# A gated recurrence of 256 steps on one core: a loop of 64 turns of 4 steps in place of 32 turns of 8

## What is computed

```python
h = silu(cond @ W1.T + b1)
gate = sigmoid(h @ W2.T + b2)[:, None, :]
# Haar levels up and down, every coefficient times gate: gives gate * x
x = x + (x + gate * x)
def step(prev_h, xw):
    next_h = tanh(prev_h @ Wh + xw)
    return next_h, next_h
xW = einsum('ntd,dh->nth', x, Wx) + b        # x: the scaled x of above
h_t = scan(step, h0=cond, xs=xW)             # 256 steps, one after the other
out = x + h_t
```

## Time and profile before

| | us |
|---|---|
| median of 3 runs (lowest, highest) | 200.63 (199.9, 201.95) |
| the profiled execution, its own time | 200.03 |
| its span, first to last instruction | 198.2 |
| TensorE matmul busy | 183.2 |
| ScalarE busy | 77.2 |
| VectorE busy | 83.0 |

### The profile page before, as it was taken

The page is one execution under the profiler, slowest core; times in us unless marked ns, Lnnn a source line. Parts: engine busy times, 40 slices in busy tenths (PEclk is TensorE's granted clock), DMA queues, the critical chain, the costliest instruction groups (busy, mean ns, idle before and its releaser), DMA issues.

```text
span 198.2 us, 25465 instructions
## 1 busy us (share of the span) xinstructions
PE 183.2 (92%) x12218; PEld 151.3 (76%) x12218; DVE 83.0 (42%) x267; ACT 77.2 (39%) x520; POOL 0.5 (0%) x5
## 2 busy tenths in 40 slices
PE   7776999999999999999999999999999999999996
PEld 4665888777778877777887777788777778887775
DVE  1632444444435344444434343444434343444441
ACT  4222333444444333444444433344444433334442
POOL 1000000000000000000000000000000000000000
DMA  5403999942002020201102020110202010020212
GB/s 161 168 7 88 318 408 416 379 197 106 0 26 80 0 107 0 106 0 45 61 0 106 2 107 0 61 45 0 106 0 106 0 77 31 0 106 0 107 53 53
DMA packets 6961, 17.99 MB, mean 91 GB/s; under 512 B 1443, under 2 KB 2726, under 8 KB 6950
## 3 DMA queue, kind: packets, MB, share of 16 engines
q1 hardware_dynamic: 6800, 17.71, 24.0%
q10 hardware_dynamic: 150, 0.15, 0.2%
HBM read 9.48 MB, written 8.39 MB: 90 GB/s over the span
## 4 chain that ended last, share of the span: by engine, by line
PE 90%; ACT 3%; issue 2%; DMA 2%; SPq 1%
PE bank_e L185 54%; PE bank_l L185 36%; ACT h_ring L172 3%; DMA wh_sb<-in_wh 2%; SPq L125 0%; SPq L124 0%; SPq L123 0%; SPq L122 0%
## 5 line engine op out<-in xcount | busy, mean ns | idle before, releaser
L185 PE MATMUL bank_e<-h_ring,wh_sb 128*32 128x32 f32 x4096 | 101.5, 201 | 8.1 <-ACT h_ring L172 8.1
L185 PEld LDWEIGHTS bank_e<-h_ring,wh_sb 128*32 128x32 f32 x4096 | 72.9, 110 | 37.6 <-ACT h_ring L172 24.4
L185 PE MATMUL bank_l<-h_ring,wh_sb 128*32 128x32 f32 x4096 | 96.2, 196 | 1.8 <-issue 1.8
L172 ACT ACTIVATE h_ring<-bank_e 128x32 f32<-128x32 f32 x256 | 50.6, 198 | 115.0 <-PE bank_e L185 115.0
L315 DVE TENSOR_TENSOR x<-x,h_ring 128x128 f32<-128x128 f32 x129 | 37.6, 291 | 106.0 <-ACT h_ring L172 106.0
L185 PEld LDWEIGHTS bank_l<-h_ring,wh_sb 128*32 128x32 f32 x4096 | 74.6, 113 | 1.9 <-issue 1.9
L185 PE MATMUL bank_l<-x_ring,wx_sb 128*32 128x64 f32 x2080 | 66.3, 224 | 0.7 <-issue 0.7
L185 PE MATMUL bank_e<-x_ring,wx_sb 128*32 128x128 f32 x1040 | 57.4, 282 | 0.0
L172 ACT ACTIVATE h_ring<-bank_l 128x32 f32<-128x32 f32 x256 | 50.2, 196 | 0.2 <-PE bank_l L185 0.2
L185 PEld LDWEIGHTS bank_l<-x_ring,wx_sb 128*32 128x32 f32 x2080 | 46.4, 111 | 0.9 <-issue 0.8
L185 PE MATMUL bank_l<-ones,b_parts 128*32 128x64 bf16 x520 | 31.6, 194 | 0.0
(11 more groups left out here) (25 smaller groups left out, 9.7 us busy)
## 6 DMA issues: line engine op xcount, KB each, us to landing
x<-in_x SPq DMA_DIRECT2D x15, 512.0 KB, 9.7
out_dram<-x SPq DMA_DIRECT2D x15, 512.0 KB, 3.0
x<-in_x SPq DMA_DIRECT2D x1, 384.0 KB, 5.0
w_t<-in_w SPq DMA_DIRECT2D x1, 256.0 KB, 3.2
wx_sb<-in_wx SPq DMA_DIRECT2D x1, 256.0 KB, 4.5
wh_sb<-in_wh SPq DMA_DIRECT2D x1, 256.0 KB, 4.5
out_dram<-x SPq DMA_DIRECT2D x1, 256.0 KB, 2.1
w_t<-in_w_cond SPq DMA_DIRECT2D x1, 145.0 KB, 2.8
```

Source lines behind the costliest of these rows:

```text
L172: nc.scalar.activation(h_ring[:, m, s * B:(s + 1) * B], z_of(s, m), ACT.Tanh)\
L185: done = nc.tensor.matmul(out[q:q + 32], weights[:, q:q + 32], moving, start=start, stop=stop, skip_group_check=True)
```

## The change

TURN is 4 and PART is 2: the loop has 64 turns of 4 steps, `x_ring` and `h_ring` hold 4 steps, and a part is 2 steps. `bank_l` has one bank for each of the 4 steps in place of two steps to a bank, so that second halves are laid one step (32 columns) at a time, and first halves 2 steps (64 columns) at a time. The pairs of fill in steps 0 to 3 are 0, 40, 32, 48. ScalarE waits, before every even step from step 4 on, until VectorE has added the h that it will overwrite. SyncE waits once, for h of step 4, and then issues chunks 1 to 15. VectorE's order within a turn is new. The first part of x that SyncE loads (`FIRST`) is 64 columns in place of 128.

```diff
-    TURN, PART = 8, 4
+    TURN, PART = 4, 2
...
             part, of = divmod(s, PART)
-            return bank_l[part][of % 2][:, of // 2 * B:(of // 2 + steps) * B] if m else \
-                bank_e[part][:, of * B:(of + steps) * B]
+            return bank_l[part][of][:, 0:B] if m else bank_e[part][:, of * B:(of + steps) * B]
...
+            sp.wait_ge(h_ready[0][1], 2)
             for c in range(1, CHUNKS):
-                if c == 1:
-                    sp.wait_ge(h_ready[6][1], 1)
-                if c == 2:
-                    sp.wait_ge(h_ready[0][1], 2)
                 sp.dma_start(x1[:, c, :, :], x[:, c, :, :]).then_inc(x_loaded[c], DMA)
...
             for t in range(T):
                 s = t % TURN
+
+                if t >= TURN and t % 2 == 0:
+                    act.wait_ge(out_ready, t // 2 - 1)
                 for m in range(HALVES):
                     act.wait_ge(z_whole[m], t + 1)
...
-            lay_bias(0, 4, 0, opens=False)
-            lay_bias(0, 2, 1, opens=False)
-            lay_bias(1, 2, 1)
+            lay_bias(0, 2, 0, opens=False)
+            lay_bias(0, 1, 1, opens=False)
+            lay_bias(1, 1, 1)
...
-                    done = lay_input(0, 2 if m else 4, k, m)
+                    done = lay_input(0, 1 if m else 2, k, m)
...
             def fill(s, turn):
                 if s == 1:
                     pe.wait_ge(input_ready[1], turn)
-                    lay_bias(4, 4, 0)
-                    lay_input(4, 4, 0, 0)
+                    for m in range(HALVES):
+                        lay_bias(2, 2 - m, m)
+                        lay_input(2, 2 - m, 0, m)
+                        lay_input(2, 2 - m, 1, m)
                 if s == 2:
-                    lay_input(4, 4, 1, 0)
-                    lay_bias(4, 2, 1)
+                    lay_bias(3, 1, 1)
+                    lay_input(3, 1, 0, 1)
+                    lay_input(3, 1, 1, 1)
+                    lay_bias(0, 2, 0)
+                    pe.wait_ge(input_ready[0], turn)
+                    lay_input(0, 2, 0, 0)
                 if s == 3:
-                    lay_input(4, 2, 0, 1)
-                    lay_input(4, 2, 1, 1)
-                    lay_bias(5, 2, 1)
...
+                    lay_input(0, 2, 1, 0)
+                    for at in range(PART):
+                        lay_bias(at, 1, 1)
+                        lay_input(at, 1, 0, 1)
+                        lay_input(at, 1, 1, 1)
...
             for turn in range(TURNS):
...
+                t = turn * TURN
+                more = turn + 1 < TURNS
+                dve.wait_ge(h_ready[0 if turn else 1][1], turn + 1)
+                if more:
+                    if (t + TURN) % CS == 0:
+                        dve.wait_ge(x_loaded[(t + TURN) // CS], DMA)
+                    scale(turn + 1, 0, in_place=False).then_inc(input_ready[0], 1)
+                else:
+                    nc.vector.memset(x_ring[:, :, 0:PART * B], 0.0).then_inc(input_ready[0], 1)
+                dve.wait_ge(x1_ready, 2 * turn + 1)
+                dve.wait_ge(h_ready[1][1], turn + 1)
+                add_out(t)
+                if more:
+                    dve.wait_ge(input_ready[0], turn + 1)
+                    scale(turn + 1, 0, in_place=True).then_inc(x1_ready, 1)
+                dve.wait_ge(x1_ready, 2 * turn + 2)
+                if more:
+                    dve.wait_ge(h_ready[3][1], turn + 1)
+                    add_out(t + 2)
+                    scale(turn + 1, 1, in_place=False).then_inc(input_ready[1], 1)
+                    dve.wait_ge(input_ready[1], turn + 2)
+                    scale(turn + 1, 1, in_place=True).then_inc(x1_ready, 1)
```

More of the change, by code:

```diff
@@ L204, in lay_input @@
             def lay_input(s, steps, k, m):
[L205 to L208, removed]
+                return by_columns(z_of(s, m, steps), wx_sb[:, k, m * P:(m + 1) * P],
+                                  x_ring[:, k, s * B:(s + steps) * B])
             def recur(s, k, m, h, start=False):
@@ L244, in _ @@
                         pe.wait_ge(first_input_ready, k + 1)
-                    done = lay_input(0, 2 if m else 4, k, m)
+                    done = lay_input(0, 1 if m else 2, k, m)
                 done.then_inc(z_whole[m], 1)
             for k in range(HALVES):
-                lay_input(1, 2, k, 1)
+                lay_input(1, 1, k, 1)
             def fill(s, turn):
@@ L254, in fill @@
                     pe.wait_ge(input_ready[1], turn)
-                    lay_bias(4, 4, 0)
-                    lay_input(4, 4, 0, 0)
+                    for m in range(HALVES):
+                        lay_bias(2, 2 - m, m)
+                        lay_input(2, 2 - m, 0, m)
+                        lay_input(2, 2 - m, 1, m)
                 if s == 2:
-                    lay_input(4, 4, 1, 0)
-                    lay_bias(4, 2, 1)
-                if s == 3:
-                    lay_input(4, 2, 0, 1)
-                    lay_input(4, 2, 1, 1)
-                    lay_bias(5, 2, 1)
[L264 to L279, removed]
+                    lay_bias(3, 1, 1)
[4 more added lines that the diff above has]
+                    lay_input(0, 2, 0, 0)
+                if s == 3:
+                    lay_input(0, 2, 1, 0)
[3 more added lines that the diff above has]
+                        lay_input(at, 1, 1, 1)
             with nc.Fori(1, TURNS + 1, engines=bass.OrderedEngineSet([pe.engine]), head_slot={pe.engine: 0}) as turn:
@@ L349, in _ @@
             for turn in range(TURNS):
[L350 to L374, removed]
@@ new lines, in _ @@
+                dve.wait_ge(h_ready[1][1], turn + 1)
[10 more added lines that the diff above has]
+                    scale(turn + 1, 1, in_place=True).then_inc(x1_ready, 1)
+                else:
+                    dve.wait_ge(h_ready[2][1], TURNS)
+                    add_out(t + 2, steps=1)
+                    dve.wait_ge(h_ready[3][0], TURNS)
+                    dve.wait_ge(h_ready[3][1], TURNS)
+                    add_out(t + 3, steps=1)
```

## The result

The changed kernel takes 208.63 us (median of 6 runs, 206.96 to 209.54), the kernel before, run beside it, 200.25 (199.9 to 201.95). The ratio is 1.039, with an interval of 1.035 to 1.043. The forecast was 200.5, up to 204.2. The profiled execution took 206.96 us, the shortest of the six, with a span of 205.1; what follows explains the 6.9 us by which this span exceeds the 198.2 of before. What made the other five up to 2.5 us longer has no trace.

What follows compares the result with a forecast made beforehand. It took the chain from first-half tanh through the recurrence, 0.718 us per step, as the bound. 200.03 - 1.35 (start) + 1.3 (fills) gave 200.0 us, stated as 200.5 for the median; range 198.6 to 204.2.

Steps and rivals of the forecast that it cites:

- The step that failed: ScalarE before even steps: the added wait on out_ready is met early and falls into 0.43 us of idling; cost nothing.
- its signs of being wrong: Listed signs against the forecast: four equal periods at 0.718, a step over 0.76, ScalarE waiting for VectorE, a loop-edge gap.
- The fills: TensorE's input and bias pairs between recurrences: two of every four steps tight, 0.01 us each, +1.3 us in all.
- the fills just fit: Rival, TensorE between recurrences: narrow bias costs half, only the start counts, 199.3 us; chance 0.22.
- The trailing group: TensorE's fourth column group in wide fills: trails by 0.07 us, so the next recurrence's last group is about 0.02 late.
- recurrence unqueued: Rival, recurrence behind fill(1) and fill(3): its loads no longer wait ready, 0.035 us per tight step, 203.7 us; chance 0.21.
- The start: The loop's first turn: one instruction-fetch gap of some 1.4 us in place of two, step 6 1.35 us earlier.
- The edges: Turn ends of the loop: 32 more of them, covered, cost nothing; without cover up to 0.3 us each.
- the cover: Time to spare at a turn's end between TensorE's compare and move and the next recurrence: 0.15 us, unchanged.
- VectorE's waits and chunk 1: VectorE's scales and adds ready in time, cover 0.35 us at the tightest; chunk 1 there near 18, wanted near 19.9.
- The added pairs: TensorE's fills: 120 pairs per 4 steps in place of 120 per 8, priced only through the fills' length.
- The 8 narrow pairs: TensorE's fills: 8 pairs with 32 f32 columns take 0.063 us.

Runs made afterwards that it cites:

- kernel 1: The changed kernel with ScalarE's two waits ahead of even steps swapped, z_whole first and out_ready second: 200.82 us, ratio 0.998.
- kernel 2: The kernel before plus an always-met ScalarE wait on out_ready, placed ahead of the z_whole wait of even steps from step 8: 209.11 us, ratio 1.042.
- kernel 6: kernel 2 with ScalarE's two waits in the other order, z_whole first: 200.66 us, ratio 1.000.
- kernel 4: kernel 1 with work left out: 4 pairs of narrow bias in fill(1), 8 pairs of input product in fill(3): 199.41 us (1 run).
- kernel 8: kernel 1 with 12 narrow pairs of step 3's second half moved from fill(2) to fill(1): 205.4 us (1 run).
- kernel 5: kernel 1 with its loop body written twice, 32 turns of 2 x 4 steps, 496 pairs: 208.16 us, ratio 1.038.
- kernel 9: kernel 5 with SyncE's loads of chunks 1 to 15 held back until h of step 7 in place of step 4: 205.55 us, ratio 1.025.
- kernel 7: kernel 2 with the added out_ready wait ahead of the second half's tanh of even steps, before the z_whole wait: 203.23 us (1 run).
- kernel 10: The kernel before with chunks 1 to 15 released by h of step 4, in place of steps 6 and 8: 201.2 us, ratio 1.001.
- kernel 3: kernel 1 with fills spread: 8 bias pairs behind the turn's last recurrence, 12 narrow pairs from fill(3) to fill(2): 202.69 us, ratio 1.009.

## Why the prediction was wrong

- **The step that failed** is "ScalarE's new wait on `out_ready`: ... the wait itself falls into ScalarE's 0.43 of idling per step. Nothing." I asked whether the new wait is met in time, and it always is. I didn't ask what it does to the wait behind it. The old wait moved to an instruction of its own, and the tanh starts 0.06 us after that: 0.061 x 126 = 7.7 us. Kernels 1, 2 and 6 show it from both sides: order swapped, gone; added alone, all there. No rival named this wait, so no chance went to it; its signs of being wrong did name a step over 0.76, and 0.779 is one.
- **The fills** were charged +1.3 us and cost 0. All steps of kernel 1 are 0.718 to 0.719 and shortening the fills gains nothing (kernel 4). With 1.3 left out the sum would still have been 8 us short. The rival "the fills just fit" was right for this term. The sums themselves were good: 0.437 against the 0.44 to be had, where kernel 8 puts the edge at 0.45. The trailing group that I charged isn't seen in the time.
- **The rival "recurrence unqueued"** (203.7) would have seemed the best fit, since two steps of every four got longer by some hundredths. They were the right steps by another cause: the steps before an even one end with ScalarE's wait, and fill(1) and fill(3) lie in the same steps. Kernel 2, which has the fills of before, tells the two apart.
- **The start** was right in the part that pays: a gap behind 128 loads with one packet ahead of it, and no gap near 14.5; kernels 5 and 9 give one gap per block. Its size was 1.35 forecast, 1.11 in the kernel after and 0.6 in kernel 1 (step 6 at 16.12). Of the 0.24 missing in the kernel after, 0.12 are ScalarE's wait in steps 4 and 6, and 0.13 the later end of the gap, 12.77 for 12.64. The packet ahead of the gap begins 0.67 us behind the loop's first weight load in the kernel before (9.74 and 10.41), 0.68 behind it in the kernel after (9.62 and 10.30), and 0.61 to 0.74 in eight of the other ten traces (1.01 in kernel 4, 1.24 in kernel 6); so far it does go by the entry into the loop, as the forecast had it. The gap is 0.91 and not 1.4 because TensorE reached it later: the first two steps took 1.40 and 1.17, with groups 0.11 apart in place of 0.06 (rows at 11.12 and 11.22). In kernel 1 the gap ends at 12.95, step 3 comes 0.83 behind it (0.60 by the forecast), and the next two steps take 0.84 and 0.78: that makes up its 0.7.
- **The gap at the loop's entry** was in no sum. It differs between executions of the same TensorE program: none in the kernel before and 1.17 in kernel 2, 0.43 in the kernel after and 1.38 in kernel 1. The profile that the forecast started from was by luck the earliest of its kind: step 6 is at 16.74 there, and at 17.12, 17.29, 17.77 and 18.08 in kernels 2, 7, 6 and 10. With the short loop it is at 15.63, 16.12, 16.14, 16.69 and 16.90 (after, kernels 1, 4, 3 and 8), on the mean 1.1 us earlier. In the medians the gain doesn't show: kernel 1 is at 0.998, with an interval that includes none.
- **The edges** of the loop cost nothing, as said, in kernel 1. But the cover didn't stay: 0.07 us in place of 0.15, and kernel 3 shows that it can be spent.
- **VectorE's waits and chunk 1** cost nothing, as said.
- **The added pairs** got no price beyond their place in the fills, and rightly for the time: 3,840 pairs more moved the steady step of kernel 1 by nothing (0.718 to 0.719). The 8 narrow pairs at 0.063 us of the forecast are two for each of the four groups of 32 output partitions: the four groups start 0.007 us apart, and within one group the two starts lie 0.032 apart (103.277 and 103.309 in the kernel before).

The sum by what was measured: 200.03 - 1.11 + 0 + 7.56 (124 even steps behind step 6) + 0.5 (two single steps) = 207.0, against 206.96.

## What to carry to other kernels

Ahead of an instruction on the critical path, write the wait that comes last first, so that the instruction itself carries it, and let waits that are long met take the instruction of their own; a wait that "costs nothing since it is met" can still cost 0.06 us each time by moving another (shown here for two waits ahead of a tanh of ScalarE: steps of 0.78 in the kernel after and kernel 2, 0.72 in kernels 1 and 6). Look in the trace for queue instructions that only wait, and at *when* they start: behind the previous work it was free here (100.3 in kernel 1, 0.62 us ahead of the tanh, step 0.72), behind the releaser it was on the path (101.15 in the kernel after, 0.06 ahead of it, step 0.78). Where steps get longer in a pattern, make the one-line kernel that has only one of the changed things before reading a cause out of the coincidence.

## What was unexpected of the hardware

- Of two waits ahead of a tanh of ScalarE, the second in the program has an instruction of its own in the trace: L169, 126 times in the kernel after and in kernel 1, and L173, 124 times in kernels 2, 6 and 7, each of 0.017 us. Where it is the wait on `z_whole`, from its start to the start of the tanh behind it 0.06 us pass (101.15 to 101.21 in the kernel after; 0.059 to 0.062 in all places but one each of the kernel after and kernels 2 and 7).
- In kernel 5 the packet of instructions began at 20.99 us, while the chunks of x filled the DMA engines (100.7%), and TensorE stood for 5.27 us; with the loads held back it began at 17.50 and TensorE stood for 1.48 (kernel 9). In kernel 10 the packet was 0.26 us ahead of the first load, and the gap was 2.10 against 1.83.
- Behind the gap of 5.27 us in kernel 5 the granted clock was 0.50 (23.2 to 26.0 us), and behind those of 1.83 and 2.10 in kernels 6 and 10 it was 0.57 on the mean (18 to 22 and 18 to 20 us), with steps of 0.86 to 1.17 us in place of 0.72. The profiled execution of before had steps of 0.72 behind a gap of 1.83; what decides wasn't found.
- In the kernel after the first two steps ran at about half rate (1.40 and 1.17 us, groups of the recurrence 0.11 apart in place of 0.06) with a granted clock of 1.00 in the window's row (9.60 to 12.00). That 1.00 is no reading: the trace's first record of the clock begins at 12.0 us, and in kernel 1 at 13.8, in both about where the half rate ends; a stretch without a record counts as 1.00. Where there are records, in kernel 6, the slow first steps (1.43 and 0.95) stand beside 0.50 (8.20 to 11.40). That the clock was lower in the kernel after too is my guess from this; no record shows it. The traces of the kernel before and of kernels 3, 7 and 9 have no record at all, and the 4.0 us for four steps of kernel 9 fall under this.
- Single steps 0.1 to 0.3 us longer in the steady part: two in the kernel after and in kernel 2, one in kernel 7, none in the kernel before and in kernels 1, 3, 4, 6 and 8. The three that have them are those in which the wait on `z_whole` has an instruction of its own. In each of the three there is one place where the tanh comes 0.34 to 0.35 us behind that instruction in place of 0.06, here in the chain of the kernel after:

```profile
141.58 0.02 ACTq L169
141.60 0.32 issue
141.92 0.21 ACT h_ring L170
```

In kernel 1, 0.62 us lie between the two, so a delay like this wouldn't show there. What makes it wasn't found.
